# Cross-attention sums normalised by VectorE straight out of PSUM, with the first three value products of a head pair issued in one tile slot

## The chip, the cores and the metric

The kernel runs on one core of one Trainium2 chip. The metric is the device time of one execution in microseconds (us); the median of several runs is compared. Engines are called by their short names: PE (TensorE), DVE (VectorE), ACT (ScalarE), POOL (GpSimd), SP (SyncE).

## The reference

A decoder layer on `x` of 16 batches, 256 positions, width 128, in float32: `x += attn(layernorm(x))` (one head of width 128), then `x += xattn(layernorm(x), ctx)`, then `x += ffn(layernorm(x))`, where the last part takes the 31 positions of a sequence with the highest router weight through a small attention and MLP. Nearly all the time goes into the middle part:

```
q = (x @ Wq)            16 heads of 64;  x: (16, 256, 128)
k, v = ctx @ Wk, ctx @ Wv                ctx: (16, 1601, 96)
attn = softmax(q k^T / 8)                per head 256 x 1601
out = (attn @ v) @ Wo + bo
```

The kernel folds `Wk` into the queries and `Wv`, `Wo` into one matrix, so the scores are products of transformed queries with the raw context (96 wide), and the values are the raw context too.

## The kernel before, in words

Each of the 16 batches has 8 head pairs, and each pair goes over the 1601 context rows in 13 tiles of 124 rows (`KT`, `KP`): 16 x 8 x 13 = 1664 tiles. Per tile:

- `st` (PE, L573 and L574): scores, transposed, 124 context rows by 512 (two heads by 256 queries), as a high and a low float16 part, into PSUM bank 4 or 5 by turns. Tile n waits for `ex` of tile n-2, because it takes the same bank.
- `st` (ACT, L897): the exponential of the bank into the float32 ring `PF` (10 tiles).
- `round` and `lo`, once for two tiles: `EH` is the float16 high part of `PF` (DVE L1091, every fourth pair of tiles ACT L904), `EL` = `PF` - `EH` is the low part (POOL L1566). Both are rings of 12 tiles.
- `av` (PE, L590 and L592), eight slots after the scores (`AV_LAG`): eight matmuls add `EH` x `Ch` and `EL` x `Cl` into PSUM bank 6. The context tile has a column of ones, so column 96 of each of the four 97-column groups is the sum of the exponentials.

After the 13th tile of a pair bank 6 holds its sums. ACT copies the bank to `U` (L913, semaphore `u`), DVE takes the reciprocal of the sums of exponentials (L1144, `u_r`), and POOL multiplies into `Un` (L1574, `un`). PE may write bank 6 again once `u` is there. Two pairs make a quad: PE transposes `Un` (`turn_u`, L646), ACT takes it to `UT` (L924), PE multiplies it by the folded value matrix (`proj`, L636), DVE adds it to `X` (L1156).

Beside this stream run, in the same engines, the row maxima of the next heads (`diff` and `base` on PE at L613, `relu` on ACT at L919, `fold` on DVE at L1114), the queries of the next batch (L623, L933, L1123), its self-attention, its context, and the selection and feed-forward of earlier batches (`sel_*` and `c_*`). `sel_rank` is one such step of DVE, once for each batch: L1368 adds two small columns of counts into `rank`, L1370 compares another with a constant into `keep`, and the steps behind them build the selection from both.

The order is written out by hand. `whole_order` goes through tile slots n and appends steps with `put(n, ...)`: `st` of tile n, `av` of tile n - 8, `round`, `lo`, then what `plan` has for this slot, then the norms and turns that come due. Each engine runs its own copy of the list strictly in order; `LATER` shifts a kind of step by some slots on one engine (`norm` by 1 on DVE and by 3 on POOL). In a pair's first slot (late = 0, where late is n - 8 modulo 13) no value product stands; the slot late = 1 has two, each other slot one. The step `norm` stands two slots behind the last value product of its pair, before the shifts. The last pair of all (`LAST_SUMS`) has a form of its own: DVE reads bank 6 directly (L1131, L1134).

Of the kernel before, what the change touches and what calls it, by code (L numbers as in the profile page):

```python
# [12 lines left out]
ALU = mybir.AluOpType  # L13
# [4 lines left out]
P = 128  # L18
# [4 lines left out]
KT = 13  # L23
# [54 lines left out]
def chosen(gq):  # L78
# [20 lines left out]
            "c_rs2": -1, "c_sc": -1, "c_scat": 2, "c_thid": 1, "c_tqk": 1, "c_turn": 4, "c_val": 1,  # L99
            "ctx_lo": 1, "ln0": 1, "ln_stats0": -3, "ln_stats1": -2, "ln_stats2": -1, "norm": 1, "q": 1,  # L100
            "sa_f": 2, "sa_qk": 1, "sa_s": 1, "sel_count": 1, "sel_w": 3, "sigma": -1},
    "pool": {"c_gather": 4, "c_rs1": 1, "c_rs2": 1, "c_turn": 5, "ln_stats0": 4, "ln_stats1": -1,
            "ln_stats2": 3, "norm": 3},
}
# [105 lines left out]
def whole_order(engine):  # L210
# [4 lines left out]
    def put(n, kind, *a):  # L215
        stream.append((n + shift.get(kind, 0), len(stream), (kind, *a)))
# [3 lines left out]
    for n in range(TOTAL + AV_LAG):  # L220
# [7 lines left out]
        late = n - AV_LAG  # L228
        if late >= 1 and late % KT == 1:
            put(n, "av", late - 1)  # L230
        if late >= 0 and late % KT:
            put(n, "av", late)
        if n % 2 and ROUND_LAG <= n < TOTAL + ROUND_LAG:
            put(n, "round", n // 2 - ROUND_LAG // 2)
# [4 lines left out]
        done = n - AV_LAG - (KT - 1)  # L239
        if done >= 2 and (done - 2) % KT == 0:  # L240
            put(n, "norm", (done - 2) // KT)
        for late, step in ((-2, ("turn_u", 0)), (2, ("turn_u", 1)), (5, ("proj",))):
# [39 lines left out]
def build(nc, a, out):  # L282

    with ExitStack() as ctx:

        def sb(name, shape, dt=F32, until=ctx):
            return until.enter_context(nc.sbuf_tensor(name, shape, dt))
# [107 lines left out]
        qscale = sb("qscale", [P, 2, 4, 2])  # L395
        U = [sb(f"U{i}", [P, 4, DC + 1]) for i in range(2)]
        Un = [sb(f"Un{i}", [P, T, 4, DC]) for i in range(2)]
# [38 lines left out]
        LAST_TURN = ("turn_u", B - 1, QD - 1, 1)  # L436
        LAST_SUMS = B * HP - 1
        G2 = G[:, :, :, :].rearrange("p w (j e) c -> p w e j c", e=2)
# [82 lines left out]
        def tensor_program():  # L521
            w = Waits(pe)

            def bank_free(s):
                k = spare_place[(s.kind, *s.a)]
                if tail_from <= k < tail_from + 6:
                    w.wait_ge(sg("un_last"), 1)
                    w.wait_ge(sg("relu"), len(fold_of))
                    w.wait_ge(sg("fold"), len(fold_of))
                    w.wait_ge(sg("ex"), TOTAL)  # L530
                elif freed(s):
                    w.wait_ge(*freed(s))
                return bank_of(s)
# [17 lines left out]
            for s in order:  # L551
# [23 lines left out]
                elif k == "av":  # L575
# [8 lines left out]
                    if t == 0 and n > 0:  # L584
                        w.wait_ge(sg("u"), b * HP + hp)
                    elif t == 0:
                        w.wait_ge(sg("m_done"), 4)
# [51 lines left out]
                elif k == "turn_u":  # L639
                    b, qd, t = s.a  # L640
                    w.wait_ge(sg("un"), min(b * HP + 2 * qd + 2, LAST_SUMS))
                    if (b, qd) == (B - 1, QD - 1):
                        w.wait_ge(sg("un_last"), 1)
                    kb = bank_free(s)
# [231 lines left out]
        def scalar_program():  # L876
# [8 lines left out]
            for s in orders["act"]:  # L885
# [12 lines left out]
                elif k == "round" and (s.a[0] % 4 == 0 or s.a[0] >= LAST_PAIRS):  # L898
# [3 lines left out]
                    if n >= ERING:  # L902
                        w.wait_ge(sg("av"), n - ERING + 1)
                    act.activation(EH[:, r - 1:r + 1, :], PF[:, f - 1:f + 1, :], ACT.Copy,  # L904
                                   scale=KEEP).then_inc(sg("eh_act"), 1)
                elif k == "av":
                    n, = s.a
                    if n % KT == KT - 1 and n // KT < LAST_SUMS:
                        x = n // KT
                        w.wait_ge(sg("av"), n + 1)  # L910
                        if x >= 2:
                            w.wait_ge(sg("un"), x - 1)
                        act.activation(U[x % 2][:, :, :], PS[:, 6, 0:4 * (DC + 1)].rearrange(  # L913
                            "p (q c) -> p q c", c=DC + 1), ACT.Copy).then_inc(sg("u"), 1)
                elif k == "diff":
# [123 lines left out]
        def vector_program():  # L1039
# [43 lines left out]
            for s in orders["dve"]:  # L1083
# [32 lines left out]
                elif k == "q":  # L1116
# [3 lines left out]
                    if b >= 1:  # L1120
# [4 lines left out]
                                             op0=ALU.mult, op1=ALU.subtract).then_inc(sg("q_lo"), 1)  # L1125
                elif k == "norm" and s.a[0] == LAST_SUMS:
                    x, = s.a
                    sums = PS[:, 6, 0:4 * (DC + 1)].rearrange("p (q c) -> p q c", c=DC + 1)
                    w.wait_ge(sg("av"), TOTAL)
                    w.wait_ge(sg("un"), x - 1)  # L1130
                    dve.reciprocal(rden_u[:, x % 2, :], sums[:, :, DC]).then_inc(*own_step())  # L1131
                    w.wait_ge(*own_steps())
                    w.wait_ge(sg("ut_mm"), T * (B * QD - 2))
                    dve.tensor_tensor(  # L1134
                        Un[1][:, :, 2:4, :].rearrange("p t h c -> p h t c"),
                        sums[:, :, 0:DC].rearrange("p (h t) c -> p h t c", t=T),
                        rden_u[:, x % 2, :].rearrange("p (h t o) -> p h t o", t=T, o=1).to_broadcast([P, 2, T, DC]),
                        ALU.mult).then_inc(sg("un_last"), 1)
                elif k == "norm":
                    x, = s.a  # L1140
                    w.wait_ge(sg("u"), x + 1)
                    if x >= 2:
                        w.wait_ge(sg("un"), x - 1)
                    dve.reciprocal(rden_u[:, x % 2, :], U[x % 2][:, :, DC]).then_inc(sg("u_r"), 1)  # L1144
                elif (k, *s.a) == LAST_TURN:
# [218 lines left out]
                elif k == "sel_rank":  # L1364
                    b, = s.a
                    j = b % 2
                    w.wait_ge(sg("sel_cnt"), T * i)
                    dve.tensor_tensor_reduce(out=rank[:, j, :], in0=cnt[:, j, 0, :], in1=cnt[:, j, 2, :], scale=1.0,  # L1368
                                             scalar=0.0, op0=ALU.add, op1=ALU.add, accum_out=spill())
                    dve.tensor_scalar(keep[:, j, :], cnt[:, j, 1, :], NSEL + 0.5, None,  # L1370
                                      ALU.is_gt).then_inc(*own_step())
                    w.wait_ge(*own_steps())
# [111 lines left out]
        def pool_program():  # L1484
# [33 lines left out]
            for s in orders["pool"]:  # L1518
# [38 lines left out]
                elif k == "lo" and s.a[0] < LAST_PAIRS:  # L1557
# [6 lines left out]
                    elif n > 1:  # L1564
                        w.wait_ge(sg("m_done"), 4)
                    pool.tensor_tensor(EL[:, r - 1:r + 1, :], PF[:, f - 1:f + 1, :], EH[:, r - 1:r + 1, :],  # L1566
                                       ALU.subtract).then_inc(sg("lo_pool"), 1)
                elif k == "norm" and s.a[0] < LAST_SUMS:
                    x, = s.a
                    b, qd = x // HP, x % HP // 2  # L1570
                    w.wait_ge(sg("u_r"), x + 1)
                    w.wait_ge(sg("ut_mm"), T * max(0, b * QD + qd - 1))

                    pool.tensor_tensor(  # L1574
                        Un[qd % 2][:, :, 2 * (x % 2):2 * (x % 2) + 2, :].rearrange("p t h c -> p h t c"),
                        U[x % 2][:, :, 0:DC].rearrange("p (h t) c -> p h t c", t=T),
                        rden_u[:, x % 2, :].rearrange("p (h t o) -> p h t o", t=T, o=1).to_broadcast([P, 2, T, DC]),
                        ALU.mult).then_inc(sg("un"), 1)
                elif k == "bias":
# [135 lines left out]
```

## Time and profile before

| | before |
|---|---|
| time, median of 3 runs | 2166.11 us (2165.36 to 2169.33) |
| profiled execution, span | 2169.9 us |
| PE busy | 2103.3 us, 97% of the span |
| POOL busy | 1933.6 us, 89% |
| ACT busy | 1832.2 us, 84% |
| DVE busy | 1736.7 us, 80% |
| PE weight loads busy | 1544.3 us, 71% |
| DMA | 22.10 MB, mean 10 GB/s |

The only time that the profiled execution has of its own is its span, which lies 3.8 us above the median of the runs. "Busy" of PE counts the modelled length of pipelined matmuls, which overlap; it is not the share of time in which PE had no gap between starts. A row of waits says how long an engine (PEld is PE's weight load) stood idle in front of a line, and what released it; "issue" is a release that no other engine's record explains. In the stream the granted TensorE clock is at full speed except in one stretch of 3.4 to 6.8 us about every 520 us.

### The profile page before, as it was taken

The numbers are of one execution on the slowest core, as the hardware profiler recorded it, in microseconds if no ns is written. First come the engines' busy times: TensorE is split into PE (matmuls) and PEld (weight loads), VectorE is DVE, ScalarE is ACT, GpSimd is POOL, SyncE is SP. The second block draws the span as 40 slices with busy tenths as digits, with TensorE's granted clock in tenths as the row PEclk, the third lists the DMA queues.
The fourth block names the chain that finished last, engine by engine and source line by source line (L and its number), as shares of the span: only waits on it lengthen the run. The fifth ranks groups of instructions, "written<-read, shape, count | busy, mean of one in ns | idle before, by whom it ended". The sixth has DMA issues, their size and how long they took to land.

```text
span 2169.9 us, 58374 instructions
## 1 busy us (share of the span) xinstructions
PE 2103.3 (97%) x22087; PEld 1544.3 (71%) x22087; DVE 1736.7 (80%) x4158; ACT 1832.2 (84%) x3124; POOL 1933.6 (89%) x1127
## 2 busy tenths in 40 slices
PE   8999999999999999999999999999999999999998
PEld 4677777777777777777777777777777777777665
DVE  7778878787887888879687797878878788886764
ACT  6898898989888888998888888898878888888872
POOL 3899999999999899999899998998989999899991
PEclk9999999999999999999999999999999999999999
DMA  3110000000000000000000000000000000000000
GB/s 73 42 38 13 2 13 2 2 13 2 13 2 2 13 2 13 2 13 2 11 13 2 13 2 2 14 2 13 2 11 13 2 13 2 2 2 2 2 11 11
DMA packets 17366, 22.10 MB, mean 10 GB/s; under 512 B 5872, under 2 KB 14976, under 8 KB 17088
## 3 DMA queue, kind: packets, MB, share of 16 engines
q1 hardware_dynamic: 15984, 18.17, 3.0%
q8 instruction: 177, 2.90, 0.6%
q14 instruction: 101, 0.83, 0.1%
q10 hardware_dynamic: 1104, 0.20, 0.1%
HBM read 16.14 MB, written 2.10 MB: 8 GB/s over the span
## 4 chain that ended last, share of the span: by engine, by line
PE 76%; DVE 11%; issue 5%; ACT 5%; POOL 2%; DMA 0%; SPq 0%; DVEq 0%; ACTq 0%; POOLq 0%
PE PS L573 14%; PE PS L613 13%; PE PS L574 13%; PE PS L590 11%; PE PS L592 10%; PE PS L636 4%; DVE EH L1091 4%; PE PS L646 2%; PE PS L623 2%; DVE over L1114 2%; POOL EL L1566 2%; ACT PF L897 2%; PE PS L657 1%; ACT over L919 1%; DVE junk L1359 1%
## 5 line engine op out<-in xcount | busy, mean ns | idle before, releaser
L1566 POOL TENSOR_TENSOR EL<-PF,EH 124x1024 f16<-124x1024 f32 x828 | 1761.7, 2153 | 144.0 <-DVE EH L1091 69.4
L897 ACT ACTIVATE PF<-PS 124x512 f32<-124x512 f32 x1664 | 972.6, 602 | 203.7 <-PE PS L574 190.1
L590 PE MATMUL PS<-Ch,EH 123*128 123x97 f16 (+1 forms) x6656 | 765.8, 207 | 22.9 <-POOL EL L1566 22.2
L592 PE MATMUL PS<-Cl,EL 123*128 123x97 f16 (+1 forms) x6656 | 762.3, 207 | 0.0
L1091 DVE TENSOR_SCALAR_CACHE_REDUCE EH<-PF 124x1024 f16<-124x1024 f32 x621 | 746.1, 1209 | 18.1 <-ACT PF L897 16.9
L590 PEld LDWEIGHTS PS<-Ch,EH 123*128 123x128 f16 (+1 forms) x6656 | 609.1, 98 | 181.5 <-issue 62.7
L1114 DVE CUSTOM_DVE_ANT_1 over<-over,PS 128x806 f32<-128x806 f32 x512 | 506.6, 989 | 284.7 <-ACT over L919 142.8
L592 PEld LDWEIGHTS PS<-Cl,EL 123*128 123x128 f16 (+1 forms) x6656 | 597.8, 98 | 168.2 <-issue 1.9
L573 PE MATMUL PS<-AH,ChT 97*124 97x512 f16 x1664 | 646.6, 389 | 6.5 <-ACT PF L897 5.8
L574 PE MATMUL PS<-AL,ClT 96*124 96x512 f16 x1664 | 633.7, 381 | 0.0
L919 ACT ACTIVATE over<-PS 128x806 f32<-128x806 f32 x512 | 433.4, 846 | 28.6 <-PE PS L613 8.6
L573 PEld LDWEIGHTS PS<-AH,ChT 97*124 97x124 f16 x1664 | 224.9, 135 | 106.0 <-ACT PF L897 42.5
L613 PE MATMUL PS<-ChT,AH 96*128 96x403 f16 x1024 | 261.8, 337 | 1.3 <-DVE pmax L1114 1.0
L613 PE MATMUL PS<-KD,AH 96*128 96x403 f16 x1024 | 261.6, 336 | 1.5 <-ACT over L919 1.2
L574 PEld LDWEIGHTS PS<-AL,ClT 96*124 96x124 f16 x1664 | 226.6, 136 | 30.4
L904 ACT ACTIVATE EH<-PF 124x1024 f16<-124x1024 f32 x211 | 223.4, 1060 | 0.0
L1123 DVE SCALAR_TENSOR_TENSOR AL<-PS,qscale,AH 96x512 f16<-96x512 f32 x128 | 95.3, 745 | 44.8 <-ACT AH L933 44.8
L1574 POOL TENSOR_TENSOR Un<-U,rden_u 128x384 f32<-128x384 f32 x127 | 112.3, 884 | 18.0 <-DVE rden_u L1144 18.0
L933 ACT ACTIVATE AH<-PS,qscale 96x512 f16<-96x512 f32 x128 | 87.5, 684 | 21.5 <-PE PS L623 20.7
L636 PE MATMUL PS<-M,UT 128*128 128x128 f32 x768 | 100.6, 281 | 0.5
L613 PEld LDWEIGHTS PS<-ChT,AH 96*128 96x128 f16 x1024 | 79.1, 98 | 19.2 <-DVE pmax L1114 4.1
L636 PEld LDWEIGHTS PS<-M,UT 128*128 128x128 f32 x768 | 90.8, 192 | 1.3 <-DVE VX L1424 0.8
(248 smaller groups left out, 1766.9 us busy)
## 6 DMA issues: line engine op xcount, KB each, us to landing
Cf<-in_ctx SPq DMA_DIRECT2D x16, 546.0 KB
X<-in_x SPq DMA_DIRECT2D x16, 128.0 KB, 2.4
out_x<-X SPq DMA_DIRECT2D x16, 128.0 KB, 1.7
msk<-in_attention_mask SPq DMA_DIRECT2D x4, 256.0 KB, 4.3
AH<-mh SPq DMA_DIRECT2D x63, 2.0 KB
Cf<-in_ctx SPq DMA_DIRECT2D x16, 53.6 KB
xWqT<-in_xWqT SPq DMA_DIRECT2D x2, 256.0 KB, 6.5
xWo<-in_xWo SPq DMA_DIRECT2D x2, 256.0 KB, 4.3
```

Of the source, the lines that this page charges most:

```text
L573: pe.matmul(o, ChT[j][:, t, :], AH[:, cs], start=True, stop=False)
L574: pe.matmul(o, ClT[j][:, t, :], AL[:, cs], start=False, stop=True).then_inc(sg("st"), 1)
L590: pe.matmul(PS[:, 6, u0:u0 + DC + 1], EH[0:kr, r, qs], Ch[j][0:kr, t, :], start=(t == 0 and q == 0), stop=False, skip_group_check=True)
L592: m = pe.matmul(PS[:, 6, u0:u0 + DC + 1], EL[0:kr, r, qs], Cl[j][0:kr, t, :], start=False, stop=(t == KT - 1), skip_group_check=True)
L613: m = pe.matmul(PS[:, bank + n, 0:NKEY], AH[0:DC, ht * P:(ht + 1) * P], src[:, n * NKEY:(n + 1) * NKEY], start=True, stop=True)
L636: m = pe.matmul(PS[:, kb, t * D:(t + 1) * D], UT[:, t, c, :], M[:, qd * QC + c, :], start=(c == 0), stop=(c == QC - 1))
L897: act.activation(PF[:, n % PRING, :], PS[0:KP, 4 + n % 2, :], ACT.Exp).then_inc(sg("ex"), 1)
L904: act.activation(EH[:, r - 1:r + 1, :], PF[:, f - 1:f + 1, :], ACT.Copy, scale=KEEP).then_inc(sg("eh_act"), 1)
L919: act.activation(over[:, i % 2, :, :], PS[:, 2:4, 0:NKEY], ACT.Relu).then_inc(sg("relu"), 1)
L1091: dve.tensor_scalar(EH[:, r - 1:r + 1, :], PF[:, f - 1:f + 1, :], KEEP, None, ALU.mult, ALU.add, accum_out=esum[:, r // 2:r // 2 + 1]).the ...
L1114: dve.tensor_tensor_reduce(out=o, in0=o, in1=PS[:, 0:2, 0:NKEY], scale=1.0, scalar=LEAST, op0=ALU.add, op1=ALU.max, accum_out=pmax[:, b % ...
L1566: pool.tensor_tensor(EL[:, r - 1:r + 1, :], PF[:, f - 1:f + 1, :], EH[:, r - 1:r + 1, :], ALU.subtract).then_inc(sg("lo_pool"), 1)
```

## The change

The sums no longer go through `U`. DVE waits for the last value product of the pair, takes the reciprocal from bank 6 and multiplies bank 6 into `Un` itself, as the last pair did before. PE may write the bank again once `un` is there. The step stands in the slot of the last value product, with no shift, and directly behind it in the order. The first two value products of a pair stand in the slot of the third (late = 2), behind its scores: slots late = 0 and late = 1 have none, late = 2 has three. ACT and POOL have no part in `norm` any more. In `sel_rank`, the add of two columns is now two one-column instructions with a column as scalar operand, and both these and the comparison have an accumulated output (into `unread`, which nobody reads).

```diff
-            "ctx_lo": 1, "ln0": 1, ..., "ln_stats2": -1, "norm": 1, "q": 1,
+            "ctx_lo": 1, "ln0": 1, ..., "ln_stats2": -1, "q": 1,
-            "ln_stats2": 3, "norm": 3},
+            "ln_stats2": 3},
 # whole_order
-        if late >= 1 and late % KT == 1:
+        if late >= 2 and late % KT == 2:
+            put(n, "av", late - 2)
             put(n, "av", late - 1)
-        if late >= 0 and late % KT:
+        if late >= 0 and late % KT >= 2:
             put(n, "av", late)
+        if late >= 0 and late % KT == KT - 1 and late // KT < B * HP - 1:
+            put(n, "norm", late // KT)
-        if done >= 2 and (done - 2) % KT == 0:
-            put(n, "norm", (done - 2) // KT)
 # PE, before the first value product of a pair
-                        w.wait_ge(sg("u"), b * HP + hp)
+                        w.wait_ge(sg("un"), b * HP + hp)
 # ACT
-                elif k == "av":
-                    ...
-                        act.activation(U[x % 2][:, :, :], PS[:, 6, 0:4 * (DC + 1)]..., ACT.Copy).then_inc(sg("u"), 1)
 # DVE
+                elif k == "norm":
                     x, = s.a
+                    b, qd = x // HP, x % HP // 2
                     sums = PS[:, 6, 0:4 * (DC + 1)].rearrange("p (q c) -> p q c", c=DC + 1)
+                    w.wait_ge(sg("av"), (x + 1) * KT)
+                    dve.reciprocal(rden_u[:, x % 2, :], sums[:, :, DC]).then_inc(sg("u_r"), 1)
+                    w.wait_ge(sg("u_r"), x + 1)
+                    w.wait_ge(sg("ut_mm"), T * max(0, b * QD + qd - 1))
                     dve.tensor_tensor(
+                        Un[qd % 2][:, :, 2 * (x % 2):2 * (x % 2) + 2, :].rearrange("p t h c -> p h t c"),
                         sums[:, :, 0:DC].rearrange("p (h t) c -> p h t c", t=T),
                         rden_u[:, x % 2, :]....to_broadcast([P, 2, T, DC]),
+                        ALU.mult).then_inc(sg("un"), 1)
-                    dve.reciprocal(rden_u[:, x % 2, :], U[x % 2][:, :, DC]).then_inc(sg("u_r"), 1)
 # DVE, sel_rank
-                    dve.tensor_tensor_reduce(out=rank[:, j, :], in0=cnt[:, j, 0, :], in1=cnt[:, j, 2, :], ...)
-                    dve.tensor_scalar(keep[:, j, :], cnt[:, j, 1, :], NSEL + 0.5, None,
-                                      ALU.is_gt).then_inc(*own_step())
+                    for t in range(T):
+                        dve.tensor_scalar(rank[:, j, t:t + 1], cnt[:, j, 0, t:t + 1], cnt[:, j, 2, t:t + 1], None,
+                                          ALU.add, ALU.add, accum_out=spill())
+                    dve.tensor_scalar(keep[:, j, :], cnt[:, j, 1, :], NSEL + 0.5, None, ALU.is_gt, ALU.add,
+                                      accum_out=spill()).then_inc(*own_step())
 # POOL
-                elif k == "norm" and s.a[0] < LAST_SUMS:
-                    ...
-                    pool.tensor_tensor(Un[qd % 2]..., U[x % 2]..., rden_u..., ALU.mult).then_inc(sg("un"), 1)
```

## Rows read from the trace of the kernel before

**Rows 1.** The page, busy time of each engine (us, share of the span, instructions).
```profile
PE 2103.3 (97%) x22087; PEld 1544.3 (71%) x22087; DVE 1736.7 (80%) x4158; ACT 1832.2 (84%) x3124; POOL 1933.6 (89%) x1127
```

**Rows 2.** Waits from 150 to 2100 us: who waited for whom, us, times, longest.
```profile
ACT PF L897 <- PE PS L574: 175.4, 339, 3.3
DVE over L1114 <- ACT over L919: 131.0, 88, 2.9
POOL EL L1566 <- DVE EH L1091: 64.8, 71, 2.2
...
PEld PS L573 <- ACT PF L897: 37.1, 126, 0.7
...
PE PS L590 <- POOL EL L1566: 21.3, 35, 1.1
...
PEld PS L724 <- issue: 6.7, 14, 0.5
...
PEld PS L657 <- issue: 5.5, 14, 0.4
...
PEld PS L590 <- ACT U L913: 3.1, 16, 0.2
```

**Rows 3.** The instructions on `U`: durations in ns, minimum, median, maximum.
```profile
L913 ACT ACTIVATE U<-PS x127: 467/487/518, 66.8 to 2118.0; 128x388 f32<-128x388 f32 x127
L1144 DVE RECIPROCAL rden_u<-U x127: 162/173/179, 70.2 to 2118.5; 128x4 f32<-128x4 f32 x127
L1574 POOL TENSOR_TENSOR Un<-U,rden_u x127: 817/827/1344, 71.1 to 2119.5; 128x384 f32<-128x384 f32 x127
```

**Rows 4.** DVE in order of time near the end: the last pair's sums.
```profile
2127.70 0.18 DVE L1131 RECIPROCAL rden_u<-PS 128x4 f32<-128x4 f32 x1 [1.04 <-PE PS L592]
2127.92 0.56 DVE L1134 TENSOR_TENSOR Un<-PS,rden_u 128x384 f32<-128x384 f32 x1
```

**Rows 5.** Five lines of DVE, durations in ns as in rows 3.
```profile
L1370 DVE TENSOR_SCALAR keep<-cnt x16: 164/2166/2171, 232.4 to 2139.1; 128x2 f32<-128x2 f32 x16
```
```profile
L1368 DVE CUSTOM_DVE_ANT_0 rank<-cnt x16: 161/700/718, 231.8 to 2139.0; 128x2 f32<-128x2 f32 x16
```
```profile
L1377 DVE TENSOR_SCALAR_CACHE_REDUCE GT<-slots,rank x32: 241/244/247, 234.6 to 2139.4; 128x32 f32<-128x32 f32 x32
```
```profile
L1107 DVE TENSOR_TENSOR KD<-ChT x16: 570/1610/1811, 21.2 to 1950.3; 96x806 f16<-96x806 f16 x16
```
```profile
L1156 DVE TENSOR_TENSOR X<-PS,X x64: 417/421/426, 109.2 to 2131.4; 128x256 f32<-128x256 f32 x64
```

**Rows 6.** Busy us of each engine in two stretches of the eighth batch.
```profile
981.50:996.50 15.00, 14.28 (x154) 10.40 (x153) 14.45 (x51) 13.07 (x22) 11.91 (x9) 1.00 0.01 2
...
1012.00:1024.00 12.00, 11.89 (x129) 8.30 (x126) 10.90 (x20) 11.00 (x19) 12.00 (x7) 1.00 0.01 3
```

**Rows 7.** POOL in order of time from 984 to 1003 us.
```profile
988.88 4.23 POOL L1566 TENSOR_TENSOR EL<-PF,EH 124x1024 f16<-124x1024 f32 x2 [2.20 <-DVE EH L1091]
...
994.13 2.13 POOL L1566 TENSOR_TENSOR EL<-PF,EH 124x1024 f16<-124x1024 f32 x1
996.21 0.83 POOL L1574 TENSOR_TENSOR Un<-U,rden_u 128x384 f32<-128x384 f32 x1
997.00 6.32 POOL L1566 TENSOR_TENSOR EL<-PF,EH 124x1024 f16<-124x1024 f32 x3
```

**Rows 8.** DVE in order of time in the same stretch.
```profile
989.45 1.21 DVE L1091 TENSOR_SCALAR_CACHE_REDUCE EH<-PF 124x1024 f16<-124x1024 f32 x1
```

**Rows 9.** ACT in order of time behind the last value product of that pair.
```profile
988.62 0.49 ACT L913 ACTIVATE U<-PS 128x388 f32<-128x388 f32 x1
989.26 1.08 ACT L897 ACTIVATE PF<-PS 124x512 f32<-124x512 f32 x2 [0.15 <-PE PS L574]
```

**Rows 10.** PE there: the scores of two slots, of which the first has no value product.
```profile
988.62 0.38 PE L573 MATMUL PS<-AH,ChT 97*124 97x512 f16 x1
988.84 0.38 PE L574 MATMUL PS<-AL,ClT 96*124 96x512 f16 x1
989.06 0.38 PE L573 MATMUL PS<-AH,ChT 97*124 97x512 f16 x1
```

More of the change, by code:

```diff
@@ L99 @@
             "c_rs2": -1, "c_sc": -1, "c_scat": 2, "c_thid": 1, "c_tqk": 1, "c_turn": 4, "c_val": 1,
-            "ctx_lo": 1, "ln0": 1, "ln_stats0": -3, "ln_stats1": -2, "ln_stats2": -1, "norm": 1, "q": 1,
+            "ctx_lo": 1, "ln0": 1, "ln_stats0": -3, "ln_stats1": -2, "ln_stats2": -1, "q": 1,
             "sa_f": 2, "sa_qk": 1, "sa_s": 1, "sel_count": 1, "sel_w": 3, "sigma": -1},
     "pool": {"c_gather": 4, "c_rs1": 1, "c_rs2": 1, "c_turn": 5, "ln_stats0": 4, "ln_stats1": -1,
-            "ln_stats2": 3, "norm": 3},
+            "ln_stats2": 3},
 }
@@ L395, in build @@
         qscale = sb("qscale", [P, 2, 4, 2])
-        U = [sb(f"U{i}", [P, 4, DC + 1]) for i in range(2)]
         Un = [sb(f"Un{i}", [P, T, 4, DC]) for i in range(2)]
@@ L436, in build @@
         LAST_TURN = ("turn_u", B - 1, QD - 1, 1)
-        LAST_SUMS = B * HP - 1
         G2 = G[:, :, :, :].rearrange("p w (j e) c -> p w e j c", e=2)
@@ L526, in bank_free @@
                 if tail_from <= k < tail_from + 6:
-                    w.wait_ge(sg("un_last"), 1)
+                    w.wait_ge(sg("un"), B * HP)
                     w.wait_ge(sg("relu"), len(fold_of))
@@ L640, in tensor_program @@
                     b, qd, t = s.a
-                    w.wait_ge(sg("un"), min(b * HP + 2 * qd + 2, LAST_SUMS))
-                    if (b, qd) == (B - 1, QD - 1):
-                        w.wait_ge(sg("un_last"), 1)
+                    w.wait_ge(sg("un"), b * HP + 2 * qd + 2)
                     kb = bank_free(s)
@@ L905, in scalar_program @@
                                    scale=KEEP).then_inc(sg("eh_act"), 1)
-                elif k == "av":
[L907 to L914, printed above, removed]
                 elif k == "diff":
@@ L1125, in vector_program @@
                                              op0=ALU.mult, op1=ALU.subtract).then_inc(sg("q_lo"), 1)
-                elif k == "norm" and s.a[0] == LAST_SUMS:
+                elif k == "norm":
                     x, = s.a
+                    b, qd = x // HP, x % HP // 2
                     sums = PS[:, 6, 0:4 * (DC + 1)].rearrange("p (q c) -> p q c", c=DC + 1)
[L1129 to L1133, printed above, removed]
+                    w.wait_ge(sg("av"), (x + 1) * KT)
+                    dve.reciprocal(rden_u[:, x % 2, :], sums[:, :, DC]).then_inc(sg("u_r"), 1)
+                    w.wait_ge(sg("u_r"), x + 1)
+                    w.wait_ge(sg("ut_mm"), T * max(0, b * QD + qd - 1))
                     dve.tensor_tensor(
-                        Un[1][:, :, 2:4, :].rearrange("p t h c -> p h t c"),
+                        Un[qd % 2][:, :, 2 * (x % 2):2 * (x % 2) + 2, :].rearrange("p t h c -> p h t c"),
                         sums[:, :, 0:DC].rearrange("p (h t) c -> p h t c", t=T),
                         rden_u[:, x % 2, :].rearrange("p (h t o) -> p h t o", t=T, o=1).to_broadcast([P, 2, T, DC]),
[L1138 to L1143, printed above, removed]
-                    dve.reciprocal(rden_u[:, x % 2, :], U[x % 2][:, :, DC]).then_inc(sg("u_r"), 1)
+                        ALU.mult).then_inc(sg("un"), 1)
                 elif (k, *s.a) == LAST_TURN:
@@ L1367, in vector_program @@
                     w.wait_ge(sg("sel_cnt"), T * i)
-                    dve.tensor_tensor_reduce(out=rank[:, j, :], in0=cnt[:, j, 0, :], in1=cnt[:, j, 2, :], scale=1.0,
-                                             scalar=0.0, op0=ALU.add, op1=ALU.add, accum_out=spill())
-                    dve.tensor_scalar(keep[:, j, :], cnt[:, j, 1, :], NSEL + 0.5, None,
-                                      ALU.is_gt).then_inc(*own_step())
+                    for t in range(T):
[3 more added lines that the diff above has]
+                                      accum_out=spill()).then_inc(*own_step())
                     w.wait_ge(*own_steps())
@@ L1567, in pool_program @@
                                        ALU.subtract).then_inc(sg("lo_pool"), 1)
-                elif k == "norm" and s.a[0] < LAST_SUMS:
[L1569 to L1578, printed above, removed]
                 elif k == "bias":
```

## The prediction

> **What bounds the kernel now.** I read the busy times first, then the waits of the stream, then single stretches of one batch in order of time. The busy times show PE at 97% of the span, POOL at 89, ACT at 84, DVE at 80 [rows 1]. That makes PE the bound, but with pipelined matmuls 97% hides small stalls, so the waits decide. There the reader sees two directions. ACT waits 175.4 us for PE's scores and DVE 131.0 us for ACT's part of the maxima: both mostly follow PE. Against it stand PE's own waits: 21.3 us in 35 pieces for POOL's low parts in front of value products, 37.1 us in front of the scores' weight load for ACT's exponentials (part of it lies beside a matmul that still runs), and 6.7 and 5.5 us in front of the transposes of L724 and L657, once a batch each (14 times) [rows 2]. Bank 6, the place where the change is made, costs PE 3.1 us today [rows 2]. So all that this change can win is stalls that come indirectly, by POOL, ACT or DVE having more time: at most about 21.3 + 37.1 + 6.7 + 5.5 = 71 us if all of it went, and much of that has other causes.
>
> Then the stretches. POOL's 64.8 us of waiting for DVE's `EH`, up to 2.2 us at a time [rows 2], says that where POOL is late, DVE is often late before it. The eighth batch shows it: from 981.5 to 996.5 us DVE is busy 14.45 of 15 us [rows 6], POOL starves 2.20 us for `EH` and then runs one instruction behind the other [rows 7]. In this stretch the stall of PE for POOL falls, once in every batch.
>
> **Part 1, the work taken from ACT and POOL.** ACT loses 127 copies of 0.487 us, 62 us; POOL loses 127 multiplies of 0.827 us, 105 us [rows 3]. Nothing of it is on PE's path by itself. POOL's relief has to be followed in the stretch where it binds. Before: `EL` 988.88 to 993.11 (two), a small root, `EL` 994.13 to 996.26, `Un` 996.21 to 997.04, `EL` from 997.00 [rows 7]. After: DVE's norm lies ahead of the `EH` of 989.45 [rows 8] and takes what the last pair's took, 0.18 us with the multiply starting 0.22 us behind its start and lasting 0.56, 0.78 us in all less some overlap with the next instruction, say 0.70 [rows 4]. `EH` then ends at 989.45 + 0.70 + 1.21 = 991.36 instead of 990.66. The second `EL` of the two began when the first ended, near 988.88 + 2.12 = 991.00; it now begins near 991.36 + 0.14 (the release takes about that) = 991.50, 0.5 to 0.56 us late. The root and the next `EL` follow late by as much, to 996.8. There `Un` is gone (0.83 with its start), so the next `EL` begins at 996.8 instead of 997.00. Net: 0.13 to 0.2 us a batch, 2 to 3 us in 16 batches. **I take -2.** If DVE were not in the way it would be up to the whole 21.3; if the lateness of 0.56 is not won back, 16 x 0.56 = +9. ACT's relief falls right behind the last value product, in front of two exponentials [rows 9]. Of the 37.1 us it can touch what lies in the first slots of a pair, where the copy stands ahead of the exponential; those are 3 of 13 slots, and part of the wait is hidden: 0 to 8.6 us, **I take -4**.
>
> **Part 2, what DVE gets.** DVE gains 127 x (0.70 - 0.09 for the reciprocal that goes, which overlapped its neighbour), 77 us. `sel_rank` gives back: `keep` takes 2.166 us at the median though it has two elements, and 0.164 at its least; `rank` 0.700 against 0.161 [rows 5]. The least of both is the last batch, when POOL is idle. An instruction with an accumulated output takes 0.241 to 0.247 us in all 32 cases, POOL busy or not [rows 5], so the three new ones come to at most 3 x 0.244 = 0.73 instead of 2.87 us: 2.1 us in each of 15 batches, 32 us. DVE's sum so rises by 45 us to about 1782, 82% of the span, and is not the bound as a sum. In the stretch that matters, the norms of three pairs fall into the part of a batch in which DVE is full, and `sel_rank` falls between the second and the third: 3 x 0.61 more, 2.1 less. Behind it DVE is earlier by 2.1 - 2 x 0.61, about 0.9 us, and from 1012 to 1024 us it is busy 10.90 of 12 [rows 6]: this is where PE waits for the transposes of L724 (of `xn`, which DVE makes) and L657. Bounds 0 and -12.2 us; **I take half, -6**.
>
> The Trainium skill (GPSIMD Engine Reference, 1. Specifications) says that VectorE and GpSimd share SBUF interfaces, with contention for VectorE instructions in a 2-port mode or with two SBUF inputs. Rows 5 agree with it for `keep`, and `KD`, with two SBUF inputs, takes 1.610 us against 0.570 at its least. By this rule the new multiply, which has one input in PSUM, is spared, and the sum is the one below; were PSUM with SBUF to count as two, it would be that of the last rival.
>
> The rows say the same of the new multiply without any rule: its one record was made with POOL idle [rows 4], but L1156, also PSUM with SBUF, takes 417 to 426 ns in all 64 places, while POOL is busy nine tenths of the time [rows 5]. Bounds: 0.56 us, and 0.56 + 1.04 (what `KD` loses) = 1.60. I take 0.56.
>
> **Part 3, bank 6 and the order.** PE may write the bank again after the norm, 0.78 us behind the last product plus whatever DVE still has in hand: up to one `EH`, 1.21 us [rows 8]. Against that stand two slots without value products and the scores of the third: at least 3 x 0.44 us (the two scores matmuls of a slot, by the starts 988.62 and 989.06) [rows 10] and usually row maxima or transposes between them (a slot takes 2169.9 / 1664 = 1.30 us on the mean). So the wait is 0 where it was 3.1 before, or in a few pairs some tenths. Cost 0, up to 127 x 0.3 if DVE is regularly a whole `EH` behind. What queues behind DVE's new wait: DVE arrives before the last product in some pairs and then holds `EH` back by up to 2.4 us; its use comes five slots (6 us) later, and `EL` needs 2.13 of these, so it is covered except in the full stretch of part 1.
>
> The empty slots have a price of their own. PE can start scores n only when exponential n-2 is done. Two exponentials in a row take 1.08 us, 0.54 each [rows 9], two slots of bare scores 0.44 each [rows 10]. With nothing else in them PE would wait 2 x 0.10 = 0.2 us a pair, 127 x 0.2 = 25 us as the upper end; where maxima or transposes fill them, nothing. Before, one slot was bare; now a second, and ACT starts it 0.49 us earlier because the copy is gone, which covers most pairs. I take 0.2 us in two of eight pairs, 32 x 0.2 = **+6**.
>
> Nothing changes in the DMAs or in the last pair, whose form was this already.
>
> **Sum.** -2 - 4 - 6 + 6 = -6 us against the profiled 2169.9, that is 2163.9; the median of the runs lies 3.8 us lower, so I forecast **2160 us**, 0.3% faster. Its own range is 2152 to 2165.
>
> **Rivals.**
> *The cover was complete* (no change). PE's stalls for POOL and ACT come from DVE and from PE's own order; what POOL and ACT are given is idle time. For it: DVE is full in the one stretch where POOL binds [rows 6], and bank 6 cost 3.1 us. Against: L724 and L657 wait there behind DVE. Time 2162 to 2170.
> *Slack goes deep* (much faster). POOL's 105 us and ACT's 62 us put every `EL` and exponential earlier, and the 21.3 us, a third of 37.1 and the 12.2 vanish: 2166 - 21 - 12 - 12 + 6 = 2127 at the very best; half way between that and the forecast is 2143. For it: POOL, at 89%, is the busiest after PE [rows 1]. Against: rows 7, where POOL waits first.
> *DVE becomes the bound in its full stretch* (slower). Place: the norm ahead of the `EH` of 989.45. Price: 0.56 us a batch that POOL can't win back, 9 us, with the bare slots' 6 and no gain behind: 2166 + 15 = 2181. It decides from the point where DVE's idle time between two `EH` falls under 0.6 us; in the stretch above it has 0.55 in 15 us [rows 6].
> *The bare slots starve PE* in every pair: 25 us instead of 6, with the other three terms at -12 as forecast: 2166 + 13 = 2179. Against it: the copy's 0.49 us [rows 9].
> *The multiply contends with POOL*: 1.04 us more on DVE, three times a batch where DVE is full, 48 x 1.04 = 50 us: 2210. L1156 speaks against it [rows 5].
>
> **Chances.** Forecast 0.42; no change 0.25; much faster 0.13; DVE bound 0.12; bare slots 0.06; contention 0.02. A measurement of this kernel tells about 0.2%, 4.3 us, from no change. Faster: 0.34 of the forecast (to 2161.8), the 0.13, and 0.03 of the second, 0.50. Same: 0.08 + 0.22, 0.30. Slower: 0.20. The range for 8 in 10 leaves out the best of "much faster" and the far ends on the other side: 2143 to 2178.
>
> **What would show it.** ACT down by 62 us and POOL by 105; DVE up by about 45; the multiply at 0.56 and the reciprocal at 0.18 us; `keep` and `rank` near 0.24 each. PE's wait for `EL` nearly unchanged in length and still once a batch (if it is gone, the rival of the deep slack is right). The waits of L724 and L657 smaller. A new wait of L590 for DVE's `Un` under 5 us. More waits of L573 for ACT in the first three slots of a pair would show the bare slots; `EH` later than before and POOL idle behind it without a return would show DVE as the bound. The forecast is wrong if the time leaves 2152 to 2165, and its reasons are wrong if that comes without the L724 and L657 waits moving.

## The result, and the profile after

The changed kernel takes 2193.73 us (median of 4 runs, 2192.41 to 2196.62) against 2167.72 us of the kernel before beside it: ratio 1.0121, 95% interval 1.0107 to 1.0135. It is 26 us slower; the forecast was 2160, the range ended at 2178. The profiled execution has a span of 2195.4 us. One execution in the experiments below, of the kernel with the norm one slot later, was disturbed (6461.77 us) and is left out of that kernel's figures.

The first view is the page's busy time, which answers to rows 1:

```profile
PE 2115.8 (96%) x22087; PEld 1550.8 (71%) x22087; DVE 1775.6 (81%) x4333; ACT 1788.5 (81%) x2997; POOL 1832.3 (83%) x1000
```

ACT has lost 44 us and POOL 101, DVE has gained 39. So the work went where the change says. ACT lost less than the 62 us of its 127 copies, because a copy overlapped what stood beside it: such a copy of 0.51 us in the first experiment below starts at 985.98, and the next instruction of ACT 0.38 us later. Then the instructions (rows 3, 4 and 5 of before): the reciprocal and multiply out of PSUM, and the new `rank` and `keep`, durations in ns as minimum, median, maximum.

```profile
L1119 DVE RECIPROCAL rden_u<-PS x128: 169/178/185, 67.0 to 2153.2; 128x4 f32<-128x4 f32 x128
L1122 DVE TENSOR_TENSOR Un<-PS,rden_u x128: 556/557/558, 67.2 to 2153.4; 128x384 f32<-128x384 f32 x128
```
```profile
L1351 DVE TENSOR_SCALAR_CACHE_REDUCE rank<-cnt x32: 205/208/214, 233.5 to 2164.6; 128x1 f32<-128x1 f32 x32
```
```profile
L1353 DVE TENSOR_SCALAR_CACHE_REDUCE keep<-cnt x16: 146/148/151, 233.8 to 2164.7; 128x2 f32<-128x2 f32 x16
```

The multiply is as forecast, 0.556 to 0.558 us in all 128 places, POOL busy or not, and `rank` and `keep` are shorter than the 0.24 us forecast; `keep` takes 0.148 us where it took 2.166 [rows 5]. But the instructions behind them that apply `keep`, with two tensor inputs in SBUF, have become longer. The same view of it before and after:

```profile
L1381 DVE SCALAR_TENSOR_TENSOR X<-X,keep x32: 345/347/368, 234.9 to 2139.9; 128x128 f32<-128x128 f32 x32
```
```profile
L1364 DVE SCALAR_TENSOR_TENSOR X<-X,keep x32: 340/360/1759, 234.3 to 2165.5; 128x128 f32<-128x128 f32 x32
```

Of its two instructions a batch the first now takes 1.66 us at the mean, where it took 0.35; that is 21 us in the whole kernel, given back out of what `sel_rank` saved. From the start of `rank` to the end of these two DVE needs 2.82 us a batch instead of 3.79, so it gains 1.0 us there and not 2.1.

The sums of busy time don't explain the loss; the waits do. Waits of the stream, 150 to 2125 us (rows 2 of before end at 2100, the stream being shorter there):

```profile
POOL EL L1549 <- DVE EH L1079: 112.6, 136, 4.1
...
PEld PS L572 <- ACT PF L894: 50.6, 138, 0.8
...
DVE rden_u L1119 <- PE PS L591: 40.5, 44, 2.8
...
PEld PS L589 <- issue: 23.1, 43, 1.0
...
PEld PS L612 <- DVE pmax L1102: 10.7, 14, 0.8
PE PS L572 <- ACT PF L894: 10.0, 42, 0.4
...
PE PS L589 <- POOL EL L1549: 9.0, 16, 0.7
PE PS L612 <- DVE pmax L1102: 8.6, 14, 0.6
...
PEld PS L721 <- issue: 6.7, 14, 0.5
...
PEld PS L654 <- issue: 5.5, 14, 0.4
```

PE's waits for POOL halved (21.3 to 9.0, and the "issue" waits in front of the value products from 60.0 to 23.1, [rows 2]). In exchange PE waits more for ACT's exponentials in front of the scores (37.1 to 50.6 on the weight load, 10.0 on the matmul), and there is a wait that did not exist: the maxima of L612 for DVE's `pmax`, 14 times, once a batch. DVE itself now stands 40.5 us in front of its reciprocal, waiting for PE. POOL, with less to do, waits longer for `EH`: 112.6 us instead of 64.8.

For an account that adds up I took PE's matmuls one by one. For each the distance from its start to the next start is compared with the short distances (the 15th percentile) of the same kind; the rest is a gap, booked on the matmul that comes late. Over tiles 110 to 1649 the sum of short distances is 1789.6 us before and 1789.4 after, so PE's work is the same; the gaps are 138.6 and 166.3 us. The difference of 27.6 us:

| gaps in front of | before | after | difference |
|---|---|---|---|
| scores, first matmul | 18.7 | 33.7 | +15.0 (slot late = 2: 2.3 to 14.7) |
| maxima L612 (`ChT`) | 3.1 | 13.4 | +10.3 (slot 36 of a batch) |
| chosen steps, scatter and a transpose (L868, L782) | 5.9 and under 1 | 11.2 and 3.9 | +9 (slot 87) |
| value products, `EH` part (L590, after L589) | 37.1 | 23.7 | -13.4 (late = 8: 12.4 to 0.5) |
| all else | | | +7 |

Some 5 us of the 27.6 are no stalls: counted in the same way, the matmuls that ran while the granted clock was at its lower level are late by 4.8 us before and by 9.6 after, spread over the rows of the table. Outside these stretches the gaps differ by 23 us. The last section comes back to this.

**The bare slots.** ACT in order of time, slots 21 to 24 of the eighth batch, after:

```profile
979.44 0.60 ACT L894 ACTIVATE PF<-PS 124x512 f32<-124x512 f32 x1
979.92 0.85 ACT L907 ACTIVATE over<-PS 128x806 f32<-128x806 f32 x1
980.64 1.10 ACT L894 ACTIVATE PF<-PS 124x512 f32<-124x512 f32 x2
```

PE there, the scores of slots 22 and 23:

```profile
980.09 0.43 PE L572 MATMUL PS<-AH,ChT 97*124 97x512 f16 x1
...
980.58 0.49 PE L643 MATMUL PS<-ident,Un 128*128 128x128 f32 x3
981.31 0.43 PE L572 MATMUL PS<-AH,ChT 97*124 97x512 f16 x1 [0.24 <-ACT PF L894]
```

Only three transposes stand between the two and no value product, and the scores of slot 23 need an exponential that ACT could start only at 980.64, behind a ReLU of 0.85 us. Before, two value tiles stood here besides, and the 0.85 us were covered by them.

**The norm ahead of `EH` and the fold.** DVE in order of time, from the end of slot 33's value product on, after:

```profile
998.53 0.17 DVE L1119 RECIPROCAL rden_u<-PS 128x4 f32<-128x4 f32 x1
998.73 0.56 DVE L1122 TENSOR_TENSOR Un<-PS,rden_u 128x384 f32<-128x384 f32 x1
999.21 1.21 DVE L1079 TENSOR_SCALAR_CACHE_REDUCE EH<-PF 124x1024 f16<-124x1024 f32 x1
1000.34 0.08 DVE L1079 DVE_READ_ACCUMULATOR EH<-PF 124x1 f32 x1
1000.34 0.99 DVE L1102 CUSTOM_DVE_ANT_1 over<-over,PS 128x806 f32<-128x806 f32 x1
```

and PE, which needs the banks that this fold reads:

```profile
1001.39 0.52 PE L612 MATMUL PS<-ChT,AH 96*128 96x403 f16 x2 [0.61 <-DVE pmax L1102]
```

The norm takes 0.68 us ahead of the `EH` (998.53 to 999.21), the `EH` stands ahead of the fold, and the fold ends at 1001.33. From the scores of slot 33 to those of slot 42 PE takes 11.23 us, where it took 10.62.

### The profile page after: what moved, and what is told of

Read it like the earlier page. It is cut to its first block and busy times, and to the rows that moved or that the text cites. A ratio compares the mean times of both kernels' runs of the same rounds, so it can differ in the third digit from the quotient of the medians.

```text
span 2195.4 us, 57776 instructions
## 1 busy us (share of the span) xinstructions
PE 2115.8 (96%) x22087; PEld 1550.8 (71%) x22087; DVE 1775.6 (81%) x4333; ACT 1788.5 (81%) x2997; POOL 1832.3 (83%) x1000
## 5 line engine op out<-in xcount | busy, mean ns | idle before, releaser
L589 PE MATMUL PS<-Ch,EH 123*128 123x97 f16 (+1 forms) x6656 | 753.2, 208 | 10.1 <-POOL EL L1549 9.0
L591 PE MATMUL PS<-Cl,EL 123*128 123x97 f16 (+1 forms) x6656 | 749.9, 207 | 0.0
L589 PEld LDWEIGHTS PS<-Ch,EH 123*128 123x128 f16 (+1 forms) x6656 | 609.8, 98 | 141.9 <-issue 23.9
L612 PE MATMUL PS<-ChT,AH 96*128 96x403 f16 x1024 | 262.4, 337 | 10.2 <-DVE pmax L1102 9.9
L612 PE MATMUL PS<-KD,AH 96*128 96x403 f16 x1024 | 260.9, 336 | 1.5 <-ACT over L907 1.2
L612 PEld LDWEIGHTS PS<-ChT,AH 96*128 96x128 f16 x1024 | 79.2, 99 | 29.4 <-DVE pmax L1102 15.2
L612 PEld LDWEIGHTS PS<-KD,AH 96*128 96x128 f16 x1024 | 79.8, 98 | 19.3 <-ACT over L907 3.4
```

Source lines behind the costliest of these rows:

```text
L589: pe.matmul(PS[:, 6, u0:u0 + DC + 1], EH[0:kr, r, qs], Ch[j][0:kr, t, :], start=(t == 0 and q == 0), stop=False, skip_group_check=True)
L591: m = pe.matmul(PS[:, 6, u0:u0 + DC + 1], EL[0:kr, r, qs], Cl[j][0:kr, t, :], start=False, stop=(t == KT - 1), skip_group_check=True)
L612: m = pe.matmul(PS[:, bank + n, 0:NKEY], AH[0:DC, ht * P:(ht + 1) * P], src[:, n * NKEY:(n + 1) * NKEY], start=True, stop=True)
```

## The experiments

**One part at a time.** The order of the value products alone, with the old way of the sums and the old `sel_rank`:

```diff
-        if late >= 1 and late % KT == 1:
+        if late >= 2 and late % KT == 2:
+            put(n, "av", late - 2)
             put(n, "av", late - 1)
-        if late >= 0 and late % KT:
+        if late >= 0 and late % KT >= 2:
             put(n, "av", late)
```

> The kernel before with only the order changed: first three value products of a pair in slot late = 2, sums still by ACT copy, DVE reciprocal, POOL multiply. Theory 1 (bare slots: PE's scores run into ACT's exponentials): most of the loss is here, +15 to +25 us over before, in front of the scores of late = 2, and worse than in the changed kernel because ACT's copy still stands ahead of the exponentials. Theory 2 (DVE: the norm, which now waits on PE and stands ahead of EH and the maxima, makes DVE late): this kernel is within 5 us of before.

Measured: 2201.4 us, ratio 1.0151 (1.0135 to 1.0168): +32 us, more than the 15 to 25 expected, and more than the whole change. PE's waits of 150 to 2100 us:

```profile
PEld PS L574 <- ACT PF L898: 73.1, 182, 1.0
...
PE PS L574 <- ACT PF L898: 20.7, 41, 0.6
```

against 37.1 [rows 2] and, in the same view of before,

```profile
PE PS L573 <- ACT PF L897: 3.4, 12, 0.4
```

The gaps in front of the scores of late = 2 are 33.3 us, against 2.3. The same slot 23, ACT and PE:

```profile
985.98 0.51 ACT L914 ACTIVATE U<-PS 128x388 f32<-128x388 f32 x1
986.36 0.87 ACT L920 ACTIVATE over<-PS 128x806 f32<-128x806 f32 x1
987.08 1.11 ACT L898 ACTIVATE PF<-PS 124x512 f32<-124x512 f32 x2
```
```profile
987.76 0.43 PE L574 MATMUL PS<-AH,ChT 97*124 97x512 f16 x1 [0.63 <-ACT PF L898]
```

The wait is 0.63 us with ACT's copy in front and 0.24 without it, 0.39 apart, a little under the copy's 0.51. So bare slots cost 33.3 - 2.3 = 31 us of gaps in late = 2 by themselves. With the rest of the change 18.6 of them come back (33.3 to 14.7); the rows of slot 23 speak for the missing copy as the reason, but no run takes the copy away alone.

The way of the sums alone (the changed kernel with the four lines above undone and the old `sel_rank`):

> The changed kernel with the order of value products of before (two in slot late = 1) and the old sel_rank: only the way of the sums is changed. Theory 1: within 5 us of before, but for a wait of PE for bank 6 in front of the first product, up to 0.3 us a pair. Theory 2: +10 to +20 us, with the wait of PE for pmax (L612, slot 36 of a batch) and the scattered waits of the chosen steps (+9 us of gaps) as in the changed kernel.

Measured: 2191.13 us, ratio 1.0099 (1.0082 to 1.0117), +22 us. The size is near that of theory 2 (+10 to +20), but the wait is not: PE's wait for `pmax` is absent here, and the chosen steps of slot 87 have only a part of theirs. Instead PE stands in front of bank 6, in slots 35 and 74 for 0.87 and 0.80 us in nearly every batch, 31.5 us of gaps in late = 1, where theory 1 had set at most 0.3 us a pair (38 us in all). Waits of 150 to 2100 us:

```profile
PE PS L588 <- DVE Un L1121: 21.9, 31, 1.2
PEld PS L588 <- DVE Un L1121: 19.8, 35, 1.1
```

In slot 35 it is an `EH` and then the self-attention's output that DVE has ahead of the norm. DVE of this kernel in order of time:

```profile
997.69 1.22 DVE L1078 TENSOR_SCALAR_CACHE_REDUCE EH<-PF 124x1024 f16<-124x1024 f32 x1
...
999.09 0.61 DVE L1223 SCALAR_TENSOR_TENSOR X<-PS,rden,X 128x128 f32<-128x128 f32 x2
999.62 0.17 DVE L1118 RECIPROCAL rden_u<-PS 128x4 f32<-128x4 f32 x1
```

So each part of the change loses by itself, and the two are less than their sum (32 + 22 against 26): the later products hide the wait for `Un` (on the matmul 0.2 us in the changed kernel against 21.9 here), and the gaps for exponentials are smaller with the copy gone.

**`sel_rank`.** Alone on the kernel before, and left out of the changed kernel:

```diff
+                    for t in range(T):
+                        dve.tensor_scalar(rank[:, j, t:t + 1], cnt[:, j, 0, t:t + 1], cnt[:, j, 2, t:t + 1], None,
+                                          ALU.add, ALU.add, accum_out=spill())
+                    dve.tensor_scalar(keep[:, j, :], ..., ALU.is_gt, ALU.add, accum_out=spill())
```

> The kernel before with only sel_rank in accumulating form. The 2.17 us of keep and 0.70 of rank fall to 0.15 to 0.25 each, DVE is 2.2 us earlier in slot 48 of each batch. If PE's waits at L724 and L657 (slots 55 and 56) hang on that: -4 to -6 us. If the time is set elsewhere: 0 within 0.1%. In the changed kernel these two waits did not move, which speaks for 0.

> The changed kernel with the old sel_rank. If the new sel_rank pays for part of the norm's load on DVE in the full stretch: 5 to 15 us slower than the changed kernel (2199 to 2209). If not: equal to it within 0.1%.

Measured: 2166.93 us, ratio 0.9991 (0.9979 to 1.0002), and 2197.58 us, ratio 1.0132 (1.0113 to 1.0151), where the changed kernel has 1.0121. Neither comparison tells the effect from nothing: the first interval holds 1, the second pair of intervals overlap. The sum of gaps is 134.2 us against 138.6 in the first and the same within 1.1 us in the second. The gaps at L724 and L657 are the same with and without it.

The three instructions gave up 2.3 us in each batch (2.166 + 0.700 less 0.148 and 2 x 0.208), but DVE did not get them: its busy sum fell by 8.6 us in all in the first (1736.7 to 1728.1), 0.5 us a batch. The step that applies `keep` took most of it, 2.01 us at the mean for the first of its two instructions a batch, where it was 0.35. In the first kernel:

```profile
L1382 DVE SCALAR_TENSOR_TENSOR X<-X,keep x32: 340/358/2131, 232.1 to 2133.6; 128x128 f32<-128x128 f32 x32
```

From the start of `rank` to the end of that step DVE gained 0.6 us a batch in both comparisons (3.79 to 3.20 us, and 3.42 to 2.82), where the first expectation had 2.2. That 0.6 us moves neither wait is shown; whether 2 us would is not.

**The norm's place and its length.** One slot later in DVE's order:

```diff
-            "ctx_lo": 1, ..., "ln_stats2": -1, "q": 1,
+            "ctx_lo": 1, ..., "ln_stats2": -1, "norm": 1, "q": 1,
```

> The changed kernel with DVE's norm one slot later in DVE's order, so behind the EH and the maxima of its slot. If it is its place ahead of EH and maxima that makes DVE late (PE's wait for pmax at slot 36, 10 us, and the waits of the chosen steps in slot 87, 9 us), these go and the time falls by 10 to 20 us, less what PE now waits for bank 6 in front of the first product (it starts about 2.3 us behind the last one). If the norm's length is the cause wherever it stands: no gain, and a new wait of PE for Un.

Measured: 2204.4 us (median of 3 runs), ratio 1.0166 (1.0134 to 1.0197), where a fall of 10 to 20 us was one of the two expectations. The wait for `pmax` is gone from PE's waits and the gaps of slot 87 have shrunk, but PE waits for `Un` behind the `EH` and the fold, with a gap of 1.92 us in slot 36 of each batch (waits of 150 to 2120 us).

```profile
PE PS L589 <- DVE Un L1122: 32.7, 23, 2.2
```

So DVE can't serve both in this stretch: whichever stands second makes PE wait, and as stalls the two orders cost nearly the same: outside the stretches at the lower clock the gaps are 2 us less than in the changed kernel. The profiled execution is 11 us longer than the changed kernel's, and the matmuls at the lower clock account for that (late by 21 us against 9.6). The fastest run, at a mean clock of 0.996, took 2193.7 us, as the changed kernel does.

The multiply over 8 of 96 columns from the ninth pair on; the other columns of the normalised sums are left out:

```diff
+                    cols_done = DC if x < 8 else 8
                     ...
-                        sums[:, :, 0:DC].rearrange(...)
+                        sums[:, :, 0:cols_done].rearrange(...)
```

> The changed kernel; from the ninth pair on the multiply covers 8 of 96 columns (the rest of the normalised sums is left out), so that DVE's multiply shrinks from 0.56 to about 0.2 us with every wait in place. If DVE's length is what costs: the waits for pmax and in slot 87 shrink by half or more, -8 to -15 us. If the wait on the last product and the bare slots are it: under -4 us, and the 15 us in front of the scores of late = 2 stay.

Measured: 2180.67 us, ratio 1.0069 (1.0054 to 1.0084), 13 us less than the changed kernel. Waits of 150 to 2100 us:

```profile
PEld PS L572 <- ACT PF L894: 50.4, 137, 0.8
...
PE PS L572 <- ACT PF L894: 10.0, 42, 0.4
...
PEld PS L612 <- DVE pmax L1102: 5.6, 14, 0.4
...
PE PS L612 <- DVE pmax L1102: 3.5, 14, 0.3
```

The waits for `pmax` halve (19.3 to 9.1), and those for exponentials don't move (60.6 to 60.4). So about 13 us hang on the length of the multiply, and the waits of the bare slots are not among them. The 14 us that stay with it short are not the bare slots alone, though that is near their 12.4 us: half of the wait for `pmax` and about 7 us more than before in the chosen steps are in it too, and against them stand some 14 us won in front of value products.

**One product, then two.**

```diff
-        if late >= 2 and late % KT == 2:
-            put(n, "av", late - 2)
+        if late >= 1 and late % KT in (1, 2):
             put(n, "av", late - 1)
```

> The changed kernel with one value product in slot late = 1 and two in late = 2. If bare slots cost PE by the exponentials: the 15 us in front of the scores of late = 2 fall to under 5. In exchange the first product meets bank 6 one slot earlier: the wait for Un of the kernel with only the way of the sums changed (31 us of gaps in slots 35, 74 and 87) comes back, so the sum is near that kernel's, 2188 to 2193, and no placement repays it.

Measured: 2190.14 us, ratio 1.0114 (1.0099 to 1.0129), inside the 2188 to 2193 expected. The gaps in front of the scores of late = 2 fall from 14.7 to 1.5 us, those in front of the first product rise to 30.8:

```profile
PE PS L588 <- DVE Un L1121: 22.3, 32, 1.2
```

**Attempts at a faster kernel.** All on the kernel before with the new `sel_rank`. POOL's multiply at six slots instead of three (`"norm": 6` in `LATER`):

> The kernel before (sums by ACT and POOL, first two products in slot late = 1) with the new sel_rank, and POOL's multiply six slots later than its place instead of three. The wait of PE for EL in slot 42 of each batch (0.72 us, 9.4 us in 13 batches) stands behind this multiply. If it is its cause: it goes, -6 to -11 us against before. If the lateness comes back at the next EL: within 3 us of before.

Measured: 2170.41 us, ratio 1.0018 (1.0006 to 1.0030), 4 us slower. The wait of slot 42 did go, and stood in slots 44 (0.76 us a batch) and 70 instead. The lateness came back at a later `EL`, as the second expectation has it. Then the second layer norm of the self-attention out of the full stretch, `q[5] + 4, q[5] + 9` to `q[5] + 12, q[5] + 17`, on both kernels:

> The kernel before with the new sel_rank, and with the second layer norm of the self-attention (ln_stats1 on DVE and POOL, sa_n2 on DVE) moved from slots 36 and 41 of a batch to 44 and 49. Theory: PE's waits for EL in slots 40 and 42 (0.88 and 0.72 us a batch) come from DVE being full and POOL doing the root in slots 33 to 42; then both fall by more than half and the time by 8 to 18 us against before. Rival: POOL's chain of EL alone sets them, or sa_f in slot 56 becomes late behind the moved norm: under 4 us or slower.

> The changed kernel with the same move. If full DVE in slots 33 to 42 is what the norm's load meets: the wait for EL in slot 40 (9.4 us in 13 batches) goes, 8 to 15 us less than the changed kernel (2179 to 2186), while the waits for exponentials in late = 2 (15 us) and for pmax in slot 36 (10 us, ahead of the moved steps) stay. If not: equal to the changed kernel within 3 us.

Measured: 2172.86 us, ratio 1.0023 (1.0014 to 1.0031), and 2214.87 us, ratio 1.0218 (1.0202 to 1.0234). In the first the waits that were aimed at fell and the gain did not come. PE's waits of the first, 150 to 2100 us:

```profile
PE PS L590 <- POOL EL L1567: 12.2, 35, 1.1
PEld PS L623 <- DVE X L1156: 12.0, 14, 0.9
PE PS L623 <- DVE X L1156: 9.9, 14, 0.7
```

The gaps between slots 33 and 45, in 13 of the batches, fall from 28.2 to 14.5 us, and those of the next pair rise from 11.9 to 30.3: the queries of slot 53 now wait for the bank that DVE frees late, and the value products of slot 48 have a gap of their own. In the second, the wait of slot 40 goes as expected, the one for `pmax` stays as expected, and slots 50 and 53 take more than that; instead of 8 to 15 us less, it takes 21 us more than the changed kernel. Smaller moves:

> The kernel before with the new sel_rank and only sa_n2 (1.2 us of DVE) moved, from slot 41 to 45; ln_stats1 stays. By the theory that full DVE sets PE's waits wherever the load stands: the wait in slot 42 falls (EH of slot 43 and 44 earlier), the one in slot 40 stays, that of slot 53 grows less than with the move to 49: -3 to -8 us against before. If any move only carries the wait along: within 3 us.

> The same with ln_stats1 moved from slot 36 to 39 and sa_n2 from 41 to 45: POOL's root (0.9 us) and DVE's statistics (0.9 us) behind the EL of slot 40. By the theory the waits in slots 40 and 42 both fall and the next ones stay under 0.3 us: -6 to -14 us against before. If the waits are carried along: within 3 us.

Measured: 2168.66 us, ratio 1.0000 (0.9990 to 1.0009), and 2168.22 us, ratio 1.0002 (0.9993 to 1.0011). Both expected gains failed. With only `sa_n2` moved the wait of slot 42 stayed; with both moved by less, the wait of slot 40 passed to the queries of the same slot, and that of slot 42 stayed. Nothing of it beats the kernel before.

## Why the prediction was wrong

- *The bound, and where to look:* right. PE's work is unchanged and the whole difference is in its waits; the full stretch of DVE from slot 33 is where the larger new one lies.
- *Durations:* right to 0.01 us for the multiply (0.557), and short ones for `rank` and `keep`. DVE's sum rose by 39 us (45 forecast), which is near by luck: `sel_rank` gave 12 us and not 32, and, with POOL less busy, two instructions with two inputs in SBUF that the forecast left as they were, `KD` and the low part `Cl`, gave 19. The contention rival is out: 556 to 558 ns beside a busy POOL.
- *"The empty slots ... I take 0.2 us in two of eight pairs", +6:* the mechanism and even the number of pairs were right (the larger gaps are in slots 23 and 62 of a batch, 0.41 and 0.34 us), and the size was off by two: 12.4 us in late = 2. I set the two exponentials against two slots of scores, but ACT's ReLU for the maxima, 0.85 us, stands between them in such a pair (the ACT rows above). "Maxima or transposes fill them" left out the other side: the maxima that fill PE's slot bring a ReLU to ACT too, and in slot 23 the transposes did not make up for it.
- *"It is covered except in the full stretch of part 1":* this is the main step that failed. I followed DVE's lateness of 0.7 us along `EH` to `EL` to the value product, and there the numbers came true: the second `EL` of the stretch began late by half a us and the wait of slot 42 went. POOL after, in order of time:

```profile
997.95 2.13 POOL L1549 TENSOR_TENSOR EL<-PF,EH 124x1024 f16<-124x1024 f32 x1 [2.19 <-DVE EH L1079]
1000.56 2.13 POOL L1549 TENSOR_TENSOR EL<-PF,EH 124x1024 f16<-124x1024 f32 x1 [0.47 <-issue]
```

  The starts are 2.61 us apart, where two took 4.23 together [rows 7]. But the same lateness reaches PE by a second way, `EH` to fold to the bank of the maxima, and there it had no slack: +10.3 us, and +9 in the chosen steps of slot 87, which also wait for DVE. The rival *DVE becomes the bound in its full stretch*, at 0.12, had the place right, the norm ahead of that `EH`. Its price of 9 us was for another path, lateness that POOL can't win back, and POOL did win it back; that 9 is near the 10.3 of the maxima is luck. The chosen steps were missing, and I gave it too small a chance because I checked one consumer only.
- *Part 1, POOL's relief, -2:* mis-sized. The gaps in front of value products fell by 13.4 us, not 2, because the wait of slot 42 vanished whole while the delay was booked elsewhere.
- *ACT's relief, -4:* no gain of it can be seen apart from the bare slots. Against the gaps that these make, up to 18.6 us (33.3 to 14.7) come with it.
- *Bank 6, cost 0:* right for the order that was forecast. PE's wait for `Un` in front of value products is 0.2 us on the matmul and 3.2 on the weight load, under the 5 us named as a sign.
- *"I take half, -6", for what `sel_rank` gives:* wrong, 0 to -2. The step that failed first is "2.1 us in each of 15 batches": the three instructions became short, and the next one on DVE took 21 of the 32 us. The waits of L721 and L654 stand at 6.7 and 5.5 us, to the digit what they were [rows 2]. They were named as a test and failed it, with DVE about 1.0 us earlier there before the norms are counted, not 2.1.
- *Sum:* -2 - 4 - 6 + 6 should have read -13 + 15 + 10 + 9 + about 7. Of the last, part is not explained: it is spread over matmuls of all kinds. About 5 us of the whole are time at the lower clock, which the forecast had no term for.

What stays open: what releases L721 and L654, and the exact share of the chosen steps that is due to the norm's place rather than to its length (with the short multiply L868 and L782 still have 9.7 and about 3 us, with the norm one slot later the gaps of the whole slot 87 fall from 16 to 8).

## What to carry to other kernels

Work taken from two engines that wait for the bound and given to one that is full in a stretch was no gain here, though the sums of busy time say there is room (DVE 80 to 81% of the span): ask for each stretch, not for the span. An instruction that is freed of a wait can hand it to the next one: read the one behind it too before its time is counted as won. When an instruction is put in front of others on an in-order engine, follow every consumer behind it to the bound, not only the longest chain. And where two engines hand a double buffer to and fro, a slot emptied on one side can be paid for by whatever the other does in it.

## What the runs showed of the hardware

In this case the granted clock fell behind stalls of PE, though not behind each of them. In the kernel with the norm one slot later PE waits for `Un` in the fifth batch,

```profile
608.55 0.20 PE L589 MATMUL PS<-Ch,EH 124*128 124x97 f16 x1 [1.76 <-DVE Un L1122]
```

and then the clock (the number behind POOL's busy time in the windows view) is below full in both windows until 615 us:

```profile
609.00:611.50 2.50, 2.50 (x31) 1.86 (x27) 2.43 (x11) 0.42 (x1) 2.33 (x4) 0.68 0.03 7
611.50:615.00 3.50, 3.50 (x29) 2.39 (x27) 3.39 (x11) 2.07 (x4) 3.03 (x3) 0.74 0.01 2
615.00:620.00 5.00, 5.00 (x60) 3.74 (x58) 3.98 (x13) 4.30 (x9) 3.30 (x2) 1.00 0.00 0
```

The record has it at 1.2 GHz for 3.4 us there, and 52 us in all in that execution, against 14.5 us in the kernel before and 21 us in the changed kernel. Behind 150 us that execution has 17 stalls of PE of 1.7 to 2.3 us; next to 12 of them a stretch at 1.2 GHz begins, and next to 5 none. The kernel before has two such stalls and the changed kernel four, all of 1.7 us and each with such a stretch. Runs of the one kernel differ accordingly: three of them took 2193.7, 2204.4 and 2208.1 us at mean clocks of 0.996, 0.990 and 0.988. So a wait of PE near 2 us can cost more than its length, and in some runs does not. In the changed kernel this is 3 us of the 26 if the whole execution is counted (half of 6.6 us more at the lower level), and 5 us in the tiles of the account, which end ahead of the last such stretch before and behind most of it after.

`keep`, two elements a partition, took 2.166 us before at the median, which is near the length of one `EL` of POOL (2.136 at the median), and 0.148 us with an accumulated output. But then the next instruction of DVE with two tensor inputs in SBUF, `X<-X,keep`, takes up to 2.131 us (the new `sel_rank` alone) where its median was 0.347. The Trainium skill (GPSIMD Engine Reference, 1. Specifications) names contention on SBUF interfaces that GpSimd shares with VectorE, for VectorE instructions in a 2-port mode or with two SBUF inputs. `X<-X,keep` agrees with the second case, and so does the new multiply, which has one SBUF input: 558 ns at most in 128 places. That the old `keep` ran in a 2-port mode no run shows.
